# A selective-scan block: where the growth's clamp is computed, and who adds up the sixteen terms

## The reference

```
A_bar = exp(d * A)                                  # A = -exp(A_log), d = delta > 0
log_A_cum = cumsum(log(max(A_bar, 1e-10)))
A_cum = exp(log_A_cum)                              # "decay"
wcum = cumsum(d * B * x / max(A_cum_shifted, 1e-10))  # 1/max(...) is the "growth"
h = A_cum * wcum / max(A_bar, 1e-10) + h_before * A_cum
y = sum over the 16 states of C * h, plus D * x
```

## Time and profile before

| | |
|---|---|
| time, median of 3 runs | 6189.16 us (6188.1 to 6192.53) |
| span of the profiled execution | 6189.9 us (no other time is given for that execution) |
| PE busy | 5686.4 us, 92% |
| DVE busy | 5633.4 us, 91% |
| ACT busy | 3734.6 us, 60% |
| POOL busy | 2744.1 us, 44% |
| mean granted TensorE clock | 0.989 |

### The profile page before, as it was taken

How to read it: one execution, slowest core, us unless ns; L and a number is a source line. 1 busy time by engine, 2 the same in 40 slices (tenths; PEclk the granted TensorE clock), 3 DMA queues, 4 the chain that set the end, 5 groups by cost and what they waited for, 6 DMA issues and landing times.

```text
span 6189.9 us, 77161 instructions
## 1 busy us (share of the span) xinstructions
PE 5686.4 (92%) x16152; PEld 2632.6 (43%) x16152; DVE 5633.4 (91%) x7057; ACT 3734.6 (60%) x4618; POOL 2744.1 (44%) x2138
## 2 busy tenths in 40 slices
PE   5999999999999999999999999999999999999997
PEld 2444444444444444444444444444444444444443
DVE  4999999999999999999999999999999999999997
ACT  3666665665666666656666666566566666665664
POOL 2444444444444444444444444444444444444443
PEclk9999999999999999999999999999999999999998
DMA  1121121121111211211212112112121121121120
GB/s 64 11 17 19 14 17 15 14 19 13 16 18 14 17 16 14 19 15 14 19 13 17 16 14 19 15 14 19 13 16 18 14 17 15 14 19 15 14 17 11
DMA packets 157893, 104.23 MB, mean 17 GB/s; under 512 B 121008, under 2 KB 121008, under 8 KB 157488
## 3 DMA queue, kind: packets, MB, share of 16 engines
q1 hardware_dynamic: 157488, 100.71, 17.8%
HBM read 42.63 MB, written 16.78 MB: 10 GB/s over the span
## 4 chain that ended last, share of the span: by engine, by line
PE 37%; DVE 31%; issue 20%; ACT 3%; DVEq 2%; ACTq 0%; DMA 0%; SPq 0%
PE state L971 13%; DVE acc L1321 11%; PE cum L961 10%; DVE term L1311 6%; PE fbank L866 5%; DVE conv L1167 4%; DVE conv L1159 2%; PE ebank L936 2%; PE ebank L916 2%; PE fbank L879 2%; DVE xn L1277 1%; ACT xiT L568 1%; DVE dx L1222 1%; DVE delta L1213 1%; PE fbank L850 1%
## 5 line engine op out<-in xcount | busy, mean ns | idle before, releaser
L699 ACT ACTIVATE decay<-cum,neg_a 128x1024 f32<-128x1024 f32 x1024 | 1138.6, 1112 | 1944.8 <-PE cum L961 1942.4
L971 PE MATMUL state<-sources,tri_upto 128*128 128x512 f32 x4096 | 1980.6, 606 | 187.4 <-DVE term L1311 187.1
L473 POOL TENSOR_SCALAR room<-total,limit 128x1024 f32<-128x1024 f32 x1024 | 1352.8, 1321 | 1653.9 <-ACT cum L704 1448.2
L463 POOL TENSOR_SCALAR step<-delta,limit 128x1024 f32<-128x1024 f32 x1024 | 1243.4, 1214 | 1661.2 <-PE cum L961 1038.5
L961 PE MATMUL cum<-step,tri_before 128*128 128x512 f32 x4096 | 1940.7, 596 | 3.5 <-DVE sources L1298 3.5
L1311 DVE SCALAR_TENSOR_TENSOR term<-state,crow,decay 128x1024 f32<-128x1024 f32 x1024 | 1308.8, 1278 | 247.4 <-PE state L971 135.9
L1321 DVE TENSOR_TENSOR acc<-acc,term 128x1024 f32<-128x1024 f32 x1024 | 1459.2, 1425 | 0.2
L1298 DVE SCALAR_TENSOR_TENSOR sources<-cum,brow,dx 128x1024 f32<-128x1024 f32 x1024 | 1303.1, 1273 | 12.1 <-ACT cum L704 12.1
L971 PEld LDWEIGHTS state<-sources,tri_upto 128*128 128x128 f32 x4096 | 744.5, 191 | 1068.5 <-issue 941.7
L961 PEld LDWEIGHTS cum<-step,tri_before 128*128 128x128 f32 x4096 | 777.7, 192 | 941.7 <-issue 935.6
L704 ACT ACTIVATE cum<-room,pos_a 128x1024 f32<-128x1024 f32 x1024 | 1143.6, 1117 | 17.6 <-POOL room L473 2.7
(11 more groups left out here) (125 smaller groups left out, 3972.7 us busy)
## 6 DMA issues: line engine op xcount, KB each, us to landing
hfirst<-hrows SPq DMA_DIRECT2D x496, 64.0 KB, 3.9
xt<-in_x SPq DMA_DIRECT2D x64, 256.0 KB, 2.6
hrows<-term SPq DMA_DIRECT2D x1024, 4.0 KB, 1.7
xres<-in_x SPq DMA_DIRECT2D x64, 256.0 KB, 2.7
out_x<-xres SPq DMA_DIRECT2D x64, 256.0 KB, 2.1
gate_last<-gate SPq DMA_DIRECT2D x512, 0.5 KB, 2.1
win<-in_w_in SPq DMA_DIRECT2D x2, 2048.0 KB, 10.7
hrows<-hrows SPq DMA_DIRECT2D x64, 64.0 KB, 2.3
```

Source lines behind the costliest of these rows:

```text
L463: nc.gpsimd.tensor_scalar(step[s % 2][:, :], delta[t.parity][:, :], limit[:, s:s + 1], 0.0, ALU.min, ALU.max).then_inc(step_ready, 1)
L473: nc.gpsimd.tensor_scalar(room[:, :], total[:, :], limit[:, s:s + 1], 0.0, ALU.min, ALU.max).then_inc(room_ready, 1)
L699: nc.scalar.activation(decay[s % 4][:, :], cum[s % 2][:, :], ACT.Exp, scale=neg_a[:, s:s + 1]).then_inc(decay_ready, 1)
L971: last = nc.tensor.matmul(state[:, cols], tri_upto[:, :], source[s % 2][:, cols], start=True, stop=True)
```

## The change

ACT takes over the clamp: `room = relu(ln 1e10 - a * total)` and `growth = exp(ln 1e10 - room)`, which is the same number as `exp(min(a*total, ln 1e10))`. POOL's `limit_sum` is gone. DVE no longer adds each term to `acc`; after every second slot it adds the odd slot's term into the even slot's (`pair`), and POOL adds that sum to `acc` (`add_pair`). The term buffers become three: two for even slots in turn, one for all odd slots. The second norm's `xn2` now lies in the first norm's buffer `xn`, with two waits for that.

```diff
+def term_at(slot):
+    return 2 if slot % 2 else slot // 2 % 2
 # POOL
-            def limit_sum(t, s):
-                ...
-                nc.gpsimd.tensor_scalar(room[:, :], total[:, :], limit[:, s:s + 1], 0.0,
-                                        ALU.min, ALU.max).then_inc(room_ready, 1)
+            def add_pair(t, s):
+                pool.wait_ge(paired, pair_at(t, s))
+                if s == 1:
+                    pool.wait_ge(front_pool, at(FRONT_POOL, t, "skip"))
+                else:
+                    pool.wait_ge(added, pair_at(t, s - 2))
+                stand(pool)
+                sums = acc[t.parity][:, :]
+                nc.gpsimd.tensor_tensor(sums, sums, term[term_at(s - 1)][:, :], ALU.add).then_inc(added, 1)
 ...
                     if s == 0 and prev is not None:
+                        add_pair(prev, NS - 1)
                         finish(prev)
+                    if s > 0 and s % 2 == 0:
+                        add_pair(t, s - 1)
 # ACT
+            def rooms(t, s):
+                if s == 0:
+                    act.wait_ge(front_act, at(FRONT_ACT, t, "total1"))
+                user, old = before(t, s, 1)
+                if user is not None:
+                    act.wait_ge(growth_ready, slot_at(user, old))
+                nc.scalar.activation(room[:, :], total[:, :], ACT.Relu, bias=ln_top, scale=neg_a[:, s:s + 1]).then_inc(room_ready, 1)
+
             def growths(t, s):
                 act.wait_ge(decay_ready, slot_at(t, s))
                 act.wait_ge(room_ready, slot_at(t, s))
-                nc.scalar.activation(cum[s % 2][:, :], room[:, :], ACT.Exp, scale=pos_a[:, s:s + 1]).then_inc(growth_ready, 1)
+                nc.scalar.activation(cum[s % 2][:, :], room[:, :], ACT.Exp, bias=ln_top, scale=-1.0).then_inc(growth_ready, 1)
 ...
                     if s == 10 and more:
                         front_abs(nxt)
                     if more or s + 2 < NS:
+                        rooms(ahead, slot)
                         decays(ahead, slot)
 # DVE
             def norm_xn(t):
 ...
+                if t.shift(-4) is not None:
+                    dve.wait_ge(end_act, at(END_ACT, t.shift(-4), "q"))
 ...
             def term_of(t, s):
-                user, old = before(t, s, 2)
-                if user is not None:
-                    dve.wait_ge(added, slot_at(user, old))
-                    dve.wait_ge(last_saved[s % 2], ring_at(user, old))
+                if s % 2:
+                    user, old = before(t, s, 2)
+                    if user is not None:
+                        dve.wait_ge(paired, pair_at(user, old))
+                        dve.wait_ge(last_saved[1], ring_at(user, old))
+                else:
+                    user, old = before(t, s, 4)
+                    if user is not None:
+                        dve.wait_ge(added, pair_at(user, old))
 ...
-            def add(t, s):
-                ...
-                nc.vector.tensor_tensor(sums, sums, term[s % 2][:, :], ALU.add).then_inc(added, 1)
+            def pair(t, s):
+                dve.wait_ge(last_saved[0], ring_at(t, s - 1))
+                dve.wait_ge(term_ready, slot_at(t, s))
+                sums = term[term_at(s - 1)][:, :]
+                nc.vector.tensor_tensor(sums, sums, term[term_at(s)][:, :], ALU.add).then_inc(paired, 1)
 ...
-                    if s > 0:
-                        add(t, s - 1)
-                    elif prev is not None:
-                        add(prev, NS - 1)
+                    if s == 0 and prev is not None:
+                        pair(prev, NS - 1)
+                    elif s > 0 and s % 2 == 0:
+                        pair(t, s - 1)
```

More of the change, by code:

```diff
@@ L30 @@
 LN_EPS = float(np.log(np.float32(EPS)))
+LN_TOP = -LN_EPS
 NORM_EPS = 1e-5
@@ L90, in slot_at, with pair_at @@
     return tile.n * NS + slot + 1
+def pair_at(tile, slot):
+    return tile.n * (NS // 2) + slot // 2 + 1
+def term_at(slot):
+    return 2 if slot % 2 else slot // 2 % 2
 def ring_at(tile, slot):
@@ L137, in mamba_block @@
         rinv = sb("rinv", [P, KD])
-        curve = sb("curve", [P, 6])
-        square_bias, below, above, ln_join, round_up, round_back = (curve[:, i:i + 1] for i in range(6))
+        curve = sb("curve", [P, 7])
+        square_bias, below, above, ln_join, round_up, round_back, ln_top = (curve[:, i:i + 1] for i in range(7))
         xt = sb("xt", [P, D])
@@ L170, in mamba_block @@
         decay = [sb(f"decay{i}", [P, DI]) for i in range(4)]
-        term = [sb(f"term{i}", [P, DI]) for i in range(2)]
+        term = [sb(f"term{i}", [P, DI]) for i in range(3)]
         acc = [sb(f"acc{i}", [P, DI]) for i in range(2)]
@@ L185, in mamba_block @@
         x2 = sb("x2", [P, D])
-        xn2 = sb("xn2", [P, D])[:, :]
+        xn2 = xn[:, :]
         estat = sb("estat", [P, 6])
@@ L241, in mamba_block @@
         term_ready = sem("term_ready")
+        paired = sem("paired")
         added = sem("added")
@@ L339, in save_last @@
                 wait(term_ready, slot_at(t, s))
-                sp.dma_start(hmain[t.parity][s:s + 1, :], term[s % 2][P - 1:P, :]).then_inc(last_saved[s % 2], 16)
+                sp.dma_start(hmain[t.parity][s:s + 1, :], term[term_at(s)][P - 1:P, :]).then_inc(last_saved[s % 2], 16)
             def finish(t):
@@ L512, in start @@
                     limit_step(t, s)
-                for s in range(2):
-                    limit_sum(t, s)
             def body(t, more, more2):
@@ L531, in body, with end @@
                             skip(nxt)
-            whole(pool, start, body, finish)
+            def end(t):
+                add_pair(t, NS - 1)
+                finish(t)
+            whole(pool, start, body, end)
         @block.scalar
@@ L741, in start @@
                 for s in range(2):
+                    rooms(t, s)
                     decays(t, s)
@@ L1271, in end_refine, with end_scale @@
                 refine(t, esmall, end_dve, END_DVE)
-            def end_scale(t):
+            def end_scale(t, in_xn):
                 prev = t.shift(-1)
@@ L1276, in end_scale @@
                     dve.wait_ge(end_act, at(END_ACT, prev, "q"))
+                if in_xn is not None:
+                    dve.wait_ge(norm_pe, at(NORM_PE, in_xn, "xnT"))
                 done(nc.vector.tensor_scalar(xn2, x2[:, :], emv[:, 0:1], esmall[:, 4:5], ALU.subtract, ALU.mult),
@@ L1419, in body @@
                         if s == 15:
-                            end_scale(prev)
+                            end_scale(prev, t.shift(2) if more2 else None)
             def end(t):
                 term_of(t, NS - 1)
-                add(t, NS - 1)
+                pair(t, NS - 1)
                 finish(t)
@@ L1433, in end @@
                 end_refine(t)
-                end_scale(t)
+                end_scale(t, None)
                 end_out(t)
```

26 lines of the change are left out of this document (6 added, 20 removed).

## The result

The changed kernel takes 6434.96 us (median of 4 runs, 6424.08 to 6439.85) against 6188.65 us: ratio 1.0392, interval 1.0377 to 1.0407. The forecast had the sign and 1.2%; the loss is over three times that. The profiled execution has a span of 6438.1 us, 248 more than before.

What follows compares the result with a forecast made beforehand. PE's own work, 5686 us, was taken as the floor, plus PE's waits. 6189.9 - 152 (DVE waits) + 159 (ACT clamps) + 10 + 3 + 75 (clock) - 22 = 6263 us, so 6262 against the runs' median; range 6160 to 6345.

Steps and rivals of the forecast that it cites:

- the wait near 240: PE's wait for ACT before the xcT transposes in slot 10, over the run: near 240 us instead of 68.6.
- PE's own work is the floor; DVE at 91% is no bound.: Whole kernel: PE's 5686 us is the floor; DVE gives up 790 us, but only removed PE waits pay, 152 us.
- the 20 of slot 8: PE's 0.32 us wait for DVE in slot 8 goes, but lies inside ACT's chain and is no gain.
- the 29 us of slot 14: Slot 13 has no add, so `term` comes over 1 us earlier and PE's 0.45 us wait goes: 29 us gained.
- The quantized rows: PE's wait before transposing them: slot 15 has no add, ACT's `end_q` comes earlier, 27 of 34.8 us go.
- The clamp and the two of them in ACT's stretch: Slots 8 to 10: clamps of 1.24 us, two before ACT's copy; PE's wait 3.8 us, tile 2.48 longer, 159 us.
- The clock: Lower clock behind the 3.8 us wait in nine tiles of ten costs 75 us; 22 saved at the loop's turn.
- POOL has slack: the step that it must deliver is needed a slot later.: POOL loses 1353 us, gains 512 adds of 1215 us, and stays below 45% busy.
- a rival at 75 us: POOL's adds wedge into slot 14 or delay a step for `cum`, 1.2 us per tile: 6340 us, chance 0.15.
- Slots 14 and 15, 10 us: ACT's clamps there fit its waits to within 0.1 or 0.2 us: a cost of 10 us.
- The collision of POOL's add with `end_refine`: Slot 14: POOL's add and skip may get between its three operations; PE waits 0 to 1.6 us in slot 15, 0 likelier.
- the loop's turn: Slot 0 of every second tile: of PE's 2.40 us wait for DVE 1.2 go, over 29 turns 35 us.

Runs made afterwards that it cites:

- The clamp alone: The kernel before the change with only the clamp moved to ACT as relu, the adds left on DVE: 6456.62 us, ratio 1.0435.
- The filler: The changed kernel with 8 more unused 512-column products per tile on PE, in slot 10 before its wait for ACT's xcT copy: 6292.9 us, ratio 1.0169.
- the two clamps put back: The changed kernel with the clamps of slots 11 and 12 back on POOL, the other 14 of a tile on ACT: 6131.4 us, ratio 0.9911.
- POOL's order alone: The changed kernel with POOL's add of a pair one slot later, behind the next step: 6253.91 us, ratio 1.0111.
- the kernel at 5974 us: The changed kernel with clamps of slots 11 and 12 on POOL, POOL's adds a slot later, carry released before the last add: 5974.22 us, ratio 0.965.

## Why the prediction was wrong

The sign was right, and so were all the readings that it named as proof: the clamp near 1.24 us, the wait near 240, the clock below 0.98. The size was not. The loss was over three times the forecast and outside the range.

- *PE's own work is the floor; DVE at 91% is no bound.* Right. DVE gave up 538 us, 790 forecast (the adds themselves went from 1459 to 622 us, but other operations of DVE now stand behind POOL's adds), and PE's waits for it fell by 139; forecast were 145 (125 and the 20 of slot 8, which went into the other chain). But the 29 us of slot 14 brought nothing: that wait went, and PE had it again at `ct`, behind ACT. The forecast looked at what ended the wait and not at what stood behind it.
- *The quantized rows:* -27 forecast, -27.2 measured. The reason was that slot 15 has no add any more. The clamp alone, which keeps that add, has this wait at 10.6 us too, so the number is in part luck.
- *The clamp and the two of them in ACT's stretch:* 1.24 us forecast, 1.234 measured; a wait of 3.8 us forecast, 3.63 measured; 179 us forecast (159 and the 20), 165 measured. The filler and the two clamps put back show this chain by experiment.
- *The clock:* mis-sized. I took 75 us of new cost less 22 saved, 53. PE's busy time rose by 113, and this is net of some 30 us that the `state` groups lost with the waits before them (1980.6 to 1950.9). Removing the cause (filler) brought 142, putting the two clamps back 182 of busy time. What was off is the length of what follows: I counted a `cum` at the lower clock, 1.3 us, and in 27 tiles the low stretch is at least twice as long and runs past ACT's wait of 1.69 us into the `z1` product and the next.
- *POOL has slack: the step that it must deliver is needed a slot later.* This is the step that failed. POOL is idle half the time (it took 241 us more, where 138 less were forecast, since its adds take 2.79 us in the mean and not 2.37), but the add was issued in the slot in which DVE's taps follow, stood behind them, and the steps stood behind the add: 67.9 us of PE's waiting, named as a rival at 75 us and left out of the forecast. I looked at load and at one collision at a time, not at what the queue passes on. With its neighbours, that order cost 181 us.
- *Slots 14 and 15, 10 us:* right for the clamp, 0.03 us in slot 14. The collision of POOL's add with `end_refine` did come, 2.24 us instead of 0.16, but PE has no wait for it in slot 15, so that 0 for it was right. At the loop's turn 29 us of waits are left, where the forecast left 35. I did not list the release of the carry behind the last add either (25 us of PE's waits, no time).

In numbers: forecast +73 on the span, measured +248. The missing 175 are 60 of clock, 68 and 25 of waits for POOL's order, 34 at `ct` (44 less 10; most of it the slot 14 gain that did not come), 6 of `term`, less 14 at the xcT wait: 179, and 4 less in the ends and small waits. This lays the difference out by waits. What each cause was worth in time is told by the runs, and there POOL's order alone is 181 us and the clock at least 142, with an overlap.

## What to carry to other kernels

An operation moved to an engine that is 60% busy costs where that engine has no wait in front of it, not in the mean: here 14 of 16 clamps added nothing to the waits for ACT, and two cost 304 us. Find the windows in which the receiving engine is full and another waits at the end, and leave the work out of these alone. When an operation is added to an in-order queue, look at what stands behind it and at what its port may block it on; one slot later in the same queue was worth 181 us. When a TensorE wait gets longer, price the clock too: two waits of 1.6 and 1.7 us in a tile brought no low stretch here, and one of 3.1 us did. But where a wait of 3.63 us was there in any case, it was better to lay the second one into it. Before a wait is booked as a gain, look at which wait comes next on the same path.

## What the runs showed of the hardware

- The lower clock came with a single PE wait of 3.63 us, in every tile behind the first. The 217 us of useless matmuls in that wait made the kernel 142 us faster. The Trainium skill (TensorE: Matmul & The Clock Gate, HAM oscillation — how this bites in real kernels) describes such an oscillation with PE waiting for transfers; here it came from another engine's copy.
- How long it stays low differs from tile to tile at the same work: 6.8 to 13.7 us in 27 tiles, half of that or less in 36. Behind the waits of 2.3 to 2.6 us at the loop's turn before the change it fell in 17 turns of 28. In the kernel at 5974 us, with waits of 1.6 and 1.7 us in each tile, it did not fall once between the first 200 us and the last 100.
- A DVE operation of one column with two SBUF inputs takes 0.16 us, and 2.24 us when POOL's two-input add has begun just before. A series of eight DVE operations of 128 columns (2.17 us) kept POOL out until its end: the add took 4.31 us instead of 2.36, and a step, which has one input, some 3.3 instead of 1.11.
- DVE sat idle some 3.2 us at each turn of the hardware loop in both kernels. After the change the profile names nothing that ended it; before, it names an ACT `decay`, which the prediction takes for made long before. What it comes from was not tested.
